# Which engine rounds the attention weights: 20 of 30 steps on ScalarE instead of 15

## The chip, the cores and the metric

The kernel runs on one NeuronCore of one Trainium2 chip. The metric is the device time of one execution in microseconds. Three runs of the kernel before gave 1110.03, 1110.61 and 1113.11 us; the median is 1110.61 us.

## The reference, cut to what matters

One layer over 1250 nodes of 768 features: a layer norm; a graph convolution over 20000 edges and an attention, both added to the input; then a mixture of experts on the normed sum. The change is in the attention, whose weights are a polynomial instead of an exponential:

```python
xn = _layernorm(x, axis=-1)
qkv = xn @ w_qkv + b_qkv          # 12 heads of 64
q, k, v = (qkv[0] * SCALE, qkv[1], qkv[2])
A = jnp.einsum('bhnd,bhmd->bhnm', q, k)
numerator = 1.0 + A + 0.5 * A * A
attn = numerator / numerator.sum(axis=-1, keepdims=True)
out = jnp.einsum('bhnm,bhmd->bhnd', attn, v)
x = x + gnn(xn, edge_index, W, b) + (out @ w_proj + b_proj)
x = x + experts(_layernorm(x))
```

The kernel computes the numerator as ((A + 1) squared + 1) / 2; the factor 1/2 drops out in the division.

## The kernel before, in words

It is written without a scheduler: each engine has its own program, written out by hand, and they meet at semaphores. Every float32 matmul is done as three products (or two) of operands that are cut into a rounded high part (type fp32r) and the low part that is left. So everything that TensorE (PE) reads has a high and a low tile: K is cut into KHA and KLA (KHB and KLB for the odd head), Q into the two halves of MA (MB), the weights of the attention into Ph and Pl.

The stages: norm, transposes and values V, up to 141 us; the attention, in six turns of one pair of heads each (`turn(j, last)`, five in a loop and the last one apart), 141 to 626 us; hidden features, edges and projection, then the experts.

A turn has 30 steps. Step i belongs to head a, to one of three chunks of 416 or 418 query columns, and to two tiles of 125 keys. One step is this chain:

1. PE, lines 1150 and 1151: scores, four matmuls into the PSUM buffer i % 2 (`sc_done`). They wait until the square of step i - 2 has emptied it.
2. ScalarE (ACT), line 834: Pf = (scores + 1) squared (`sq_done`). It waits for the scores and, three buffers round, for Pl of step i - 3.
3. The rounding: Ph = Pf + 1 as fp32r. On ACT it is line 812 (`round_weights`); on VectorE (DVE) it is line 1022. The list `HI_ON_ACT` of line 600 says which engine does it for which step.
4. DVE, line 1024: Pl = Pf + 1 - Ph (`p_lo`), always on DVE.
5. PE, line 1166: four matmuls of Ph and Pl with the values vsb, three steps later (LAG = 3).

All engines work strictly in the order of their programs. What matters for the change is where the rounding stands there. On DVE it stands in step i, right in front of Pl(i). On ACT the rounding of step i stands in round i + 1 of the loop, behind the square of step i + 1; that square in turn waits for the scores of step i + 1.

Between these steps lies other work, put at fixed steps by tables of numbers: the next pair's projections of Q and K (PE lines 1872 to 1874; read out by ACT 767 and 770), their high parts (ACT 779, 781) and low parts (DVE 894, 898), the splitting of the next weights (ACT 759, DVE 881), comparisons of edge keys (DVE 977), the folding of the output (ACT 821, DVE 955), the denominators (DVE 948, 950), and K turned round for a Gram matrix: PE transposes it in three groups at steps 24, 27 and 30 (line 1088), ACT takes the high part one round later (786), DVE the low part two rounds later (908), all through one PSUM bank. So PE may begin a group only when DVE's line 908 has finished the one before; the Gram matrix (line 1095, step 32) waits for the third. Behind it PE begins the next pair. The turn ends on DVE with the division and splitting of the output (lines 965 to 969).

Of the kernel before, what the change touches and what calls it, by code (L numbers as in the profile page):

```python
# [70 lines left out]
STEPS = 30  # L71
# [30 lines left out]
def build(nc, x, src, dst, gnn_w, gnn_b, w_qkv, b_qkv, w_proj, b_proj, sw, sb_, w1, b1, w2, b2, out,  # L102
          counts, keyd, vdram, odram, rows, x1d, invd, blank):
    ctx = ExitStack()
    with ctx:
# [491 lines left out]
                    pe.wait_ge(xt_lo, FIRST_UNIT[4])  # L597
                value(i)

        HI_ON_ACT = [i % 5 in (1, 3) or i in (0, 27, 29) for i in range(STEPS)]  # L600
        NA = sum(HI_ON_ACT)
        ND = STEPS - NA
        FREE = 1
# [152 lines left out]
        def _(act):  # L756
# [48 lines left out]
            def turn(j, last):  # L805
                def round_weights(i):

                    w = step(i)[4]
                    act.wait_ge(sq_done, j * STEPS + (i + 1))
                    if i >= RING:  # L810
                        act.wait_ge(pv_done, j * STEPS + (i - RING + 1))
                    act.activation(Ph[:, i % RING, :, 0:w], Pf[:, i % RING, :, 0:w], ACT.Identity,  # L812
                                   bias=1.0).then_inc(p_hiA, 1)
# [14 lines left out]
                for i in range(END):  # L828
                    if i < STEPS:
                        w = step(i)[4]  # L830
                        act.wait_ge(sc_done, j * STEPS + (i + 1))
                        if i >= RING:
                            act.wait_ge(p_lo, j * STEPS + (i - RING + 1))
                        act.activation(Pf[:, i % RING, :, 0:w], ps[0:T, 2 * (i % 2):2 * (i % 2) + 2, 0:w],  # L834
                                       ACT.Square, bias=1.0).then_inc(sq_done, 1)
                    if 1 <= i <= STEPS and HI_ON_ACT[i - 1]:
                        round_weights(i - 1)
# [40 lines left out]
        def _(dve):  # L878
# [56 lines left out]
            def turn(j, last):  # L935
# [61 lines left out]
                for i in range(END):  # L997
# [15 lines left out]
                    if i < STEPS:  # L1013
                        w = step(i)[4]
                        p, f, h = Pl[:, i % RING, :, 0:w], Pf[:, i % RING, :, 0:w], Ph[:, i % RING, :, 0:w]
                        if i >= RING:
                            dve.wait_ge(pv_done, j * STEPS + (i - RING + 1))
                        if HI_ON_ACT[i]:
                            dve.wait_ge(p_hiA, j * NA + (sum(HI_ON_ACT[:i]) + 1))
                        else:  # L1020
                            dve.wait_ge(sq_done, j * STEPS + (i + 1))
                            dve.tensor_scalar(h, f, 1.0, None, ALU.add).then_inc(p_hiD, 1)  # L1022
                            dve.wait_ge(p_hiD, j * ND + (i - sum(HI_ON_ACT[:i]) + 1))
                        dve.scalar_tensor_tensor(out=p, in0=f, scalar=1.0, in1=h.bitcast(F32), op0=ALU.add,  # L1024
# [880 lines left out]
```

## Time and profile before

| | |
|---|---|
| median of the runs | 1110.61 us |
| the profiled execution | 1114.51 us, of it 1112.6 us span |
| PE matmul busy | 933.1 us (84% of the span) |
| DVE busy | 773.2 us (69%) |
| ACT busy | 483.2 us (43%) |
| 225 to 305 us (pair 1 without its last 3 us): PE, DVE, ACT busy | 73.50, 68.48, 52.76 of 80 us |
| roundings L812 on ACT / L1022 on DVE | 90 / 90 |
| where the page's 40 slices show POOL idle | from slice 23 (612 us) to the experts |
| first scores of the six pairs | 140.97, 225.01, 307.91, 392.18, 474.84, 558.81 us |
| last values matmul of the last pair starts | 625.60 us |

Pairs are counted from 0, and so are steps. Pf(25) means the square of step 25, and in the same way Ph and Pl. In a line of the profile, "PE 0.48 [1.33 <-DVE kt L908]" means that the instruction was busy for 0.48 us and that its engine had been idle for 1.33 us before it, until DVE's line 908 released it. PE matmuls overlap at their ends (one starts each 0.19 us, though one takes 0.35). Also on DVE and ACT a following instruction often starts some 0.1 us before the shown end of the one before, so that the time one instruction takes out of an engine's day is best read from start to start.

### The profile page before, as it was taken

To read this page: it belongs to the slowest core of one execution; us is meant where nothing else is said; L and a number is where in the kernel's file an instruction comes from. 1 tells how busy PE (TensorE), PEld (TensorE's weight loads), DVE (VectorE), ACT (ScalarE), POOL (GpSimd) and SP (SyncE) were. 2 spreads that over 40 slices of the span, in tenths; PEclk is the share of its full clock that TensorE was granted. 3 is DMA by queue.
4 is the path that set the end of the run, shared out by engine and by line. 5 is a ranking of instruction groups with operands and counts; after the bars stand their busy time and mean duration, and the time that the engine had idled before them with its cause. 6 is when DMAs were issued, how large, how long until landed. Compare 5 with 4: busy or idle time off the path is not lost.

```text
span 1112.6 us, 15566 instructions
## 1 busy us (share of the span) xinstructions
PE 933.1 (84%) x5250; PEld 887.4 (80%) x5250; DVE 773.2 (69%) x1557; ACT 483.2 (43%) x710; POOL 342.0 (31%) x223
## 2 busy tenths in 40 slices
PE   3897789989989989989998779699999983197885
PEld 3896778878878978878987679699999982197885
DVE  6778168889878889878887635646676666067673
ACT  2221256656656656656667402112232222154540
POOL 2025555544546546534344000000000002323342
PEclk9898899999999999999999889899999995599898
DMA  8966443283273273285463374554545424786761
GB/s 235 350 181 144 85 88 49 36 153 56 28 153 49 35 153 52 32 173 118 120 133 70 47 164 108 135 134 110 146 114 144 109 70 152 214 268 213 232 223 45
DMA packets 139572, 142.44 MB, mean 128 GB/s; under 512 B 71418, under 2 KB 119133, under 8 KB 138503
## 3 DMA queue, kind: packets, MB, share of 16 engines
q1 hardware_dynamic: 110628, 125.01, 42.7%
q0 software_dynamic: 28496, 16.68, 10.3%
q8 instruction: 26, 0.43, 0.2%
q10 hardware_dynamic: 403, 0.17, 0.1%
q14 instruction: 19, 0.16, 0.0%
HBM read 99.09 MB, written 42.97 MB: 128 GB/s over the span
## 4 chain that ended last, share of the span: by engine, by line
PE 51%; DVE 16%; issue 12%; DMA 9%; ACT 8%; POOL 1%; SPq 1%; DVEq 0%; ACTq 0%; POOLq 0%
PE ps L1872 12%; PE ps L1874 11%; PE ps L1873 11%; PE ps L1166 6%; PE ps L1150 3%; PE ps L1151 3%; ACT Ph L812 3%; DMA out<-oE,ids 3%; DVE Pl L1024 3%; DMA vdram<-VS 3%; ACT Pf L834 2%; DVE Ph L1022 2%; PE ps L1520 1%; DMA Cs<-counts 1%; DVE oE L1806 1%
## 5 line engine op out<-in xcount | busy, mean ns | idle before, releaser
L372 POOL DMA_INDIRECT counts<-countc,idxu x157 | 273.5, 1742 | 299.8 <-DMA counts<-countc,idxu 204.7
L1024 DVE SCALAR_TENSOR_TENSOR Pl<-Pf,Ph 125x832 fp32r<-125x832 f32 (+1 forms) x180 | 184.4, 1026 | 65.0 <-ACT Ph L812 58.9
L834 ACT ACTIVATE Pf<-ps 125x832 f32<-125x832 f32 (+1 forms) x180 | 155.8, 866 | 147.1 <-PE ps L1151 140.1
L1166 PE MATMUL ps<-Ph,vsb 125*128 125x416 f32 (+1 forms) x360 | 132.1, 367 | 10.4 <-DVE Pl L1024 10.1
L1166 PE MATMUL ps<-Pl,vsb 125*128 125x416 f32 (+1 forms) x360 | 127.8, 355 | 0.0
L1663 POOL DMA_INDIRECT rows<-XF,slots x10 | 14.7, 1470 | 337.3 <-DVE slots L1479 334.6
L1872 PE MATMUL ps<-XH,wqkH 128*128 128x416 f32 (+1 forms) x216 | 81.3, 376 | 19.6 <-DVE R L942 9.9
L1872 PE MATMUL ps<-wH,XH 128*125 128x384 f32 x240 | 84.7, 353 | 10.5 <-DVE OHL L969 5.8
L1166 PEld LDWEIGHTS ps<-Ph,vsb 125*128 125x128 f32 x360 | 68.9, 191 | 20.7 <-DVE Pl L1024 10.6
L1873 PE MATMUL ps<-wL,XH 128*125 128x384 f32 x240 | 83.4, 348 | 0.0
L1874 PE MATMUL ps<-wH,XL 128*125 128x384 f32 x240 | 83.2, 346 | 0.0
L812 ACT ACTIVATE Ph<-Pf 125x832 fp32r<-125x832 f32 (+1 forms) x90 | 80.0, 896 | 0.7
L1150 PE MATMUL ps<-MA,KHA 128*125 128x416 f32 (+1 forms) x180 | 70.5, 392 | 10.6 <-DVE MA L898 10.6
L1874 PE MATMUL ps<-XH,wqkL 128*128 128x416 f32 (+1 forms) x216 | 78.0, 361 | 0.0
L1873 PE MATMUL ps<-XL,wqkH 128*128 128x416 f32 (+1 forms) x216 | 77.6, 359 | 0.0
L1872 PE MATMUL ps<-HH,CH 125*125 125x384 f32 x200 | 69.5, 347 | 7.4 <-DVE CL L1358 7.4
L1166 PEld LDWEIGHTS ps<-Pl,vsb 125*128 125x128 f32 x360 | 69.3, 193 | 0.9
L1873 PE MATMUL ps<-HL,CH 125*125 125x384 f32 x200 | 68.4, 342 | 0.0
L1874 PE MATMUL ps<-HH,CL 125*125 125x384 f32 x200 | 68.3, 341 | 0.0
L1150 PE MATMUL ps<-MB,KHB 128*125 128x416 f32 (+1 forms) x180 | 65.2, 362 | 0.7 <-ACT Pf L834 0.7
L1151 PE MATMUL ps<-MA,KLA 128*125 128x416 f32 (+1 forms) x180 | 64.5, 358 | 0.0
L1151 PE MATMUL ps<-MB,KLB 128*125 128x416 f32 (+1 forms) x180 | 63.9, 355 | 0.0
(247 smaller groups left out, 2243.5 us busy)
## 6 DMA issues: line engine op xcount, KB each, us to landing
Cs<-counts SPq DMA_DIRECT2D x20, 546.9 KB
w1s<-L_ffn_w SPq DMA_DIRECT2D x8, 1152.0 KB
w2s<-L_ffn_w SPq DMA_DIRECT2D x8, 1152.0 KB, 5.7
odram<-OHL SPq DMA_DIRECT2D x12, 625.0 KB, 8.5
oS<-odram SPq DMA_DIRECT2D x10, 750.0 KB, 4.8
vdram<-VS SPq DMA_DIRECT2D x10, 672.0 KB
vsb<-vdram SPq DMA_DIRECT2D x12, 560.0 KB
kt<-keyd SPq DMA_DIRECT2D x5, 1280.0 KB, 6.0
```

The source lines that it names most:

```text
L372: pool.indirect_dma_start(out=counts, out_offset=bass.IndirectOffsetOnAxis(ap=idxu[:, c:c + 1], axis=0), in_=countc[:, c:c + 1], in_offset ...
L812: act.activation(Ph[:, i % RING, :, 0:w], Pf[:, i % RING, :, 0:w], ACT.Identity, bias=1.0).then_inc(p_hiA, 1)
L834: act.activation(Pf[:, i % RING, :, 0:w], ps[0:T, 2 * (i % 2):2 * (i % 2) + 2, 0:w], ACT.Square, bias=1.0).then_inc(sq_done, 1)
L1022: dve.tensor_scalar(h, f, 1.0, None, ALU.add).then_inc(p_hiD, 1)
L1024: dve.scalar_tensor_tensor(out=p, in0=f, scalar=1.0, in1=h.bitcast(F32), op0=ALU.add, op1=ALU.subtract).then_inc(p_lo, 1)
L1150: pe.matmul(out_, KH[a][:, kt * T:(kt + 1) * T], q, start=True, stop=False)
L1151: ins = pe.matmul(out_, KL[a][:, kt * T:(kt + 1) * T], q, start=False, stop=True)
L1166: ins = pe.matmul(ps[:, 4 + s % 2, 0:w], vsb[:, 2 * kp + t, a, :], part[:, m % RING, t, 0:w], start=(kp == 0 and t == 0 and part is Ph), s ...
L1663: pool.indirect_dma_start(out=rows, out_offset=bass.IndirectOffsetOnAxis(ap=slots[:, i:i + 1], axis=0), in_=XF[:, i, :], in_offset=None, b ...
L1872: pe.matmul(out, lh, rh, start=(k == 0), stop=False)
L1873: pe.matmul(out, lh, rl, start=False, stop=False)
L1874: ins = pe.matmul(out, ll, rh, start=False, stop=(k == tiles - 1))
```

## The change

The list that gives the rounding to ACT is replaced by a regular pattern of three:

```diff
-        HI_ON_ACT = [i % 5 in (1, 3) or i in (0, 27, 29) for i in range(STEPS)]
+        HI_ON_ACT = [i % 3 != 2 for i in range(STEPS)]
```

Before, ACT rounded steps 0, 1, 3, 6, 8, 11, 13, 16, 18, 21, 23, 26, 27, 28 and 29, 15 in all. Now it rounds all but 2, 5, 8, ... 29, which makes 20. Ten steps go from DVE to ACT (4, 7, 9, 10, 12, 15, 19, 22, 24, 25) and five from ACT to DVE (8, 11, 23, 26, 29). `NA` and `ND`, the numbers of roundings of a turn by which the semaphores count, follow from the list. PE's instructions and their order are the same in both.

ACT's part of the program for rounds 25 and 26 of a turn (Pf(25) to the first instruction behind Pf(26)), before:

```order
L834 ACTIVATE Pf<-ps 125x2x416
L758 ISA
L759 ACTIVATE wqkH<-ws 128x768
L785 ISA
L786 ACTIVATE kt<-ps 125x4x128
L779 ACTIVATE KHA<-K 64x416
L831 REGISTER_ALU
L834 ACTIVATE Pf<-ps 125x2x416
L779 ACTIVATE KHA<-K 64x416
```

and now:

```order
L834 ACTIVATE Pf<-ps 125x2x416
L812 ACTIVATE Ph<-Pf 125x2x416
L758 ISA
L759 ACTIVATE wqkH<-ws 128x768
L785 ISA
L786 ACTIVATE kt<-ps 125x4x128
L779 ACTIVATE KHA<-K 64x416
L831 REGISTER_ALU
L834 ACTIVATE Pf<-ps 125x2x416
L812 ACTIVATE Ph<-Pf 125x2x416
L779 ACTIVATE KHA<-K 64x416
```

Ph(24) now stands behind Pf(25), in front of the weights' split, and Ph(25) behind Pf(26).

DVE's part of the program for steps 25 and 26, from the low parts of step 25 to Pl(26), before:

```order
L1021 REGISTER_ALU
L1022 TENSOR_SCALAR Ph<-Pf 125x2x416
L1023 REGISTER_ALU
L1024 SCALAR_TENSOR_TENSOR Pl<-Pf,Ph 125x2x416
L893 ISA
L894 TENSOR_TENSOR KLA<-K,KHA 64x418
L908 TENSOR_TENSOR kt<-ps,kt 125x4x128
L1017 REGISTER_ALU
L1024 SCALAR_TENSOR_TENSOR Pl<-Pf,Ph 125x2x416
```

and now:

```order
L1017 REGISTER_ALU
L1019 REGISTER_ALU
L1024 SCALAR_TENSOR_TENSOR Pl<-Pf,Ph 125x2x416
L893 ISA
L894 TENSOR_TENSOR KLA<-K,KHA 64x418
L908 TENSOR_TENSOR kt<-ps,kt 125x4x128
L1021 REGISTER_ALU
L1022 TENSOR_SCALAR Ph<-Pf 125x2x416
L1023 REGISTER_ALU
L1024 SCALAR_TENSOR_TENSOR Pl<-Pf,Ph 125x2x416
```

Pl(25), and with it line 908 of the first turned group behind it, now waits for ACT's Ph(25); the rounding in front of Pl(26) has come to DVE.

DVE's program for steps 28 and 29, from Pl(28) on, now (before, the same without the row L1022 and without the counting rows round it):

```order
L1024 SCALAR_TENSOR_TENSOR Pl<-Pf,Ph 125x2x416
L908 TENSOR_TENSOR kt<-ps,kt 125x4x128
L1021 REGISTER_ALU
L1022 TENSOR_SCALAR Ph<-Pf 125x2x416
L1023 REGISTER_ALU
L1024 SCALAR_TENSOR_TENSOR Pl<-Pf,Ph 125x2x416
L954 REGISTER_ALU
L955 TENSOR_TENSOR OUN<-ps,tmpo 64x416
```

The rounding of step 29 now stands on DVE, in front of all the work that ends a turn.

## Rows read from the trace of the kernel before

**Rows 1.** Groups of instructions by line: busy us, mean ns, idle before.

```profile
L812 ACT ACTIVATE Ph<-Pf 125x832 fp32r<-125x832 f32 (+1 forms) x90 | 80.0, 896 | 0.7
L1022 DVE TENSOR_SCALAR Ph<-Pf 125x832 fp32r<-125x832 f32 (+1 forms) x90 | 56.3, 625 | 6.3 <-DVE eqp L977 2.5
```

**Rows 2.** Waits from 225 to 308 us, one pair: us in total, times, longest.

```profile
PE ps L1872 <- DVE R L942: 2.0, 1, 2.0
...
PE ps L1150 <- DVE MA L898: 1.5, 1, 1.5
...
PE ps L1088 <- DVE kt L908: 1.3, 1, 1.3
PE ps L1166 <- DVE Pl L1024: 1.2, 2, 0.8
...
PE ps L1095 <- DVE kt L908: 1.2, 1, 1.2
```

**Rows 3.** Timeline of pair 1, steps 4 and 5: start, us, engine, line.

```profile
237.95 0.54 ACT L781 ACTIVATE MA<-Q 64x416 fp32r<-64x416 f32 x1
...
238.90 1.03 DVE L1024 SCALAR_TENSOR_TENSOR Pl<-Pf,Ph 125x836 fp32r<-125x836 f32 x1
```

**Rows 4.** Timeline of pair 1, steps 15 to 17.

```profile
269.37 0.60 DVE L1022 TENSOR_SCALAR Ph<-Pf 125x836 fp32r<-125x836 f32 x1
...
269.97 0.89 ACT L812 ACTIVATE Ph<-Pf 125x836 fp32r<-125x836 f32 x1
...
271.18 0.43 PE L1166 MATMUL ps<-Ph,vsb 125*128 125x418 f32 x1 [0.47 <-DVE Pl L1024]
...
271.35 1.03 DVE L1024 SCALAR_TENSOR_TENSOR Pl<-Pf,Ph 125x836 fp32r<-125x836 f32 x1
...
275.23 0.46 PE L1166 MATMUL ps<-Ph,vsb 125*128 125x418 f32 x1 [0.77 <-DVE Pl L1024]
```

**Rows 5.** Timeline of pair 1, steps 25 to 29, ACT alone.

```profile
288.36 0.87 ACT L834 ACTIVATE Pf<-ps 125x832 f32<-125x832 f32 x1 [0.73 <-PE ps L1151]
289.12 0.84 ACT L759 ACTIVATE wqkH<-ws 128x768 fp32r<-128x768 f32 x1
...
290.33 0.54 ACT L779 ACTIVATE KHA<-K 64x416 fp32r<-64x416 f32 x1
...
293.69 0.86 ACT L834 ACTIVATE Pf<-ps 125x832 f32<-125x832 f32 x1 [1.36 <-PE ps L1151]
294.45 0.89 ACT L812 ACTIVATE Ph<-Pf 125x832 fp32r<-125x832 f32 x1
295.24 0.60 ACT L770 ACTIVATE Q<-ps,pbias 128x418 f32<-128x418 f32 x1
295.73 0.87 ACT L834 ACTIVATE Pf<-ps 125x832 f32<-125x832 f32 x1
...
299.62 1.68 ACT L812 ACTIVATE Ph<-Pf 125x832 fp32r<-125x832 f32 x2
```

**Rows 6.** Timeline of pair 1, steps 25 to 30, DVE and PE.

```profile
292.03 1.03 DVE L1024 SCALAR_TENSOR_TENSOR Pl<-Pf,Ph 125x832 fp32r<-125x832 f32 x1
...
293.48 0.68 DVE L908 TENSOR_TENSOR kt<-ps,kt 125x512 fp32r<-125x512 f32 x1
...
294.25 0.66 PE L1088 MATMUL ps<-ident,K 128*125 128x128 f32 x4
...
300.65 1.03 DVE L1024 SCALAR_TENSOR_TENSOR Pl<-Pf,Ph 125x832 fp32r<-125x832 f32 x1 [1.12 <-ACT Ph L812]
...
302.19 1.02 DVE L1024 SCALAR_TENSOR_TENSOR Pl<-Pf,Ph 125x832 fp32r<-125x832 f32 x1
...
302.33 0.48 PE L1088 MATMUL ps<-ident,K 128*125 128x128 f32 x2 [1.33 <-DVE kt L908]
```

**Rows 7.** Timeline of the last pair's end, DVE and PE.

```profile
622.91 1.96 DVE L1024 SCALAR_TENSOR_TENSOR Pl<-Pf,Ph 125x832 fp32r<-125x832 f32 x2 [0.91 <-ACT Ph L812]
...
631.71 0.65 PE L1872 MATMUL ps<-wH,XH 128*125 128x384 f32 x1 [5.77 <-DVE OHL L969]
```

## The prediction

> **What bounds the kernel now.** I read the busy times by stretch first: in one pair's 80 us PE is busy for 92% of the time, DVE for 86% and ACT for 66% (73.50, 68.48 and 52.76 us). So PE sets the length of a pair, and a moved rounding only counts where it makes PE wait or spares it a wait. The list of waits for one pair [rows 2] gives those places. PE waits for DVE five times for more than a microsecond or so in sum: for R (2.0 us) and for MA (1.5 us) at steps 5 to 7, for Pl before the value matmuls (1.2 us, of it 0.47 at step 15 and 0.77 at step 17 [rows 4]), for the second turned group of K (1.3 us, in front of L1088 at step 30) and for the third (1.2 us, in front of L1095). The reader is to see that each wait has an instruction of DVE behind it, none of ACT. That speaks for relieving DVE; but DVE in turn sat idle for ACT's Ph in front of many a Pl, as in the row at 300.65 [rows 6]. The question at each place is thus which of the two engines is late, and I followed the timeline of pair 1 step by step. Pairs 0 to 4 repeat it within a few tenths.
>
> **What a moved rounding costs by itself.** On ACT 0.896 us, on DVE 0.625 us in the mean [rows 1]. Per pair ACT gets five more, 4.5 us, and has 27 of 80 us idle; DVE loses five, 3.1 us. No engine becomes the bound by its sum. The order decides: on ACT, Ph(i) comes behind Pf(i+1), on DVE right before Pl(i).
>
> Here the Trainium skill speaks against the direction: "Trainium Architecture — The Big Picture", section "The five engines, in one table", says that ScalarE is not for simple arithmetic and that VectorE is up to about 3 times faster per element. The rows give 0.896 to 0.625, a factor of 1.4 [rows 1]. By the page's full factor, an estimate, a rounding on ACT would take 3 x 0.625 = 1.9 us, and the two that lie on the path below would delay it by some 2 us more in each of five pairs, to 1128 or so. I go by the rows.
>
> **Steps 0 to 9.** Steps 0 to 3 are unchanged. Ph(4) goes to ACT behind Pf(5), where L781 starts now, at 237.95. It ends at 237.95 + 0.90 = 238.85, and Pl(4) can start at 238.88; it starts at 238.90 now [rows 3]. So the waits for MA and R stay as they are: 0. Ph(7) and Ph(9) make Pl(7) and Pl(9) later by 0.9 and 0.3 us, which PE does not feel (their value matmuls started 4.0 and 1.3 us after Pl's end). Ph(8) on DVE makes Pl(8) 1.2 us earlier, which PE does not need either.
>
> **Steps 10 to 22.** This is where the gain is. DVE gives up Ph(15), which stands at 269.37 [rows 4], so Pl(15) is ready some 0.65 us earlier and the 0.47 us wait before the values of step 15 goes. The next in line is Pl(16). It cannot follow by 0.65: it needs ACT's Ph(16), which ended at 269.97 + 0.89 = 270.86 and is now 0.07 later, since Ph(15) and a read-out stand in front of Pf(17). Pl(16) starts at 270.96 instead of 271.35 [rows 4], 0.39 earlier, and so do Ph(17) and Pl(17), for which PE waited 0.77 [rows 4]. So of 1.24 us of waits 0.4 us is really won, the rest turns into a wait at step 17. In two pairs of five a wait of 0.12 at step 10 goes as well. I take 0.45 us per pair; the bounds are 0 and 1.3. The moved Ph(12), Ph(19), Ph(22) find ACT idle enough.
>
> **Steps 24 to 27, a new wait.** Ph(24) and Ph(25) go to ACT. Before, ACT's chain was Pf(25) at 288.36, split of the weights at 289.12, high parts until 290.33 + 0.54 = 290.87, then idle until Pf(26). Now Ph(24) starts at 289.12 and takes 0.79 of ACT's time (from start to start, as 294.45 to 295.24); split, turned K and KHA follow, 1.75 us, until 291.66; then Pf(26), and 0.76 later (as 293.69 to 294.45) Ph(25), at 292.42, which ends at 293.31 [rows 5]. Pl(25) started at 292.03 and can now start at 293.34: 1.31 us later. DVE's L908 behind it was done at 293.48 + 0.68 = 294.16, just in time for PE's L1088 at 294.25 [rows 6]. It is now done at 295.47, and L1088 starts at 295.53 (0.06 behind, as at 302.27 and 302.33). PE loses 1.28 us. PE being earlier by the 0.45 helps nothing here, since ACT's chain starts with the scores of step 25 and is earlier by as much.
>
> Does it come back? PE runs into the next wait at 301.00 (1.33 us idle before 302.33) [rows 6], which could swallow a delay. It does not: that wait ends with L908, behind Pl(28), behind ACT's Ph(28) (1.12 us idle before 300.65) [rows 6], and ACT works from Pf(28) at 295.73 to Ph(28) at 299.62 without a gap [rows 5]. Pf(28) starts with the scores of step 28, which PE issues behind the delayed L1088. So the whole chain is 1.28 later. Ph(26), which leaves ACT, stood in front of it, but Pf(28) waited for the scores anyway.
>
> **Step 29.** Ph(29) goes from ACT to DVE, behind L908 and in front of Pl(29), which now starts at 302.19 [rows 6]. From there DVE works without a gap of more than 0.16 us until the third L908, for which PE waits in front of L1095 [rows 2]. The rounding takes 0.62 us of DVE, and all of it is added: 0.62 us per pair.
>
> **The last pair.** It has no projections, so PE waits for Pl nearly throughout, and ACT and DVE take turns in being late. I followed it in the same way: in steps 7 to 22 Pl comes up to 0.6 us earlier, but the inverse of the denominators (behind Ph(13), unchanged) and the three large weight splits on both engines catch this up, and Pl(26) to Pl(28) start as now, held by ACT. At the end Ph(29) on DVE splits the two Pl [rows 7]; DVE works without a gap from there to the end of the turn, for which PE waits (5.77 us idle) [rows 7]. So +0.62; the bounds are -3.1 (all five roundings) and +3.
>
> **The sum.** 5 x (1.28 + 0.62 - 0.45) = 7.25, and 0.62 for the last pair: 7.9 us. The scatter of edges on POOL is over by 612 us (POOL's digit in the page's slices is 0 from there), before the attention ends, so it adds nothing; the stages behind the attention are the same and only start later. Against the profiled execution's 1114.5 us this makes 1122.4. That execution was 3.9 us above the median, and I take the difference over to the median: 1110.6 + 7.9 = 1118.5 us.
>
> **The rivals.**
> 1. DVE's relief wins. For it: all of PE's long waits have a DVE line behind them [rows 2]. If the waits for Pl went wholly (1.24 per pair), nothing were added at the end of a turn, and the last pair gained 3.1: -9.3, 1101.3 us. Against it: Pl(16) needs ACT, and Ph(29) is plainly added to DVE's chain.
> 2. No new wait before L1088, because ACT's queue clears in another order than I reckon, or L908 has slack. Then 5 x (0.62 - 0.45) + 0.62 = +1.5, 1112.1 us, no change that can be told. Against it: the margin now is 294.25 - 294.16 = 0.09 us.
> 3. ACT becomes late more often: nothing is won at steps 15 and 17, since each Ph now follows another Ph, and the last pair, where ACT has less slack, pays 3 us. 5 x 1.90 + 3 = +12.5, 1123.1 us. For it: in the last pair steps of PE need 1.5 us, and square and rounding on ACT 1.6.
>
> **How the numbers follow.** Forecast 0.60, rival 1 0.10, rival 2 0.17, rival 3 0.13. A measurement of this kernel can tell about 0.3%, 3.3 us. The forecast lies beyond this unless its sum is wrong by more than half, which I give a tenth of its chance or less. Slower: 0.55 + 0.13 + a little of rival 2 = 0.70; same: 0.05 + 0.14 = 0.19; faster 0.11. The range: the forecast with its bounds goes from +3 to +12; to leave out no more than a fifth it has to take in most of rival 2 and rival 3 up to its price: 1109.5 to 1124.
>
> **What would show it.** In the changed kernel's profile: 120 of L812 and 60 of L1022; in each of the five pairs a wait of about 1.3 us of PE before the L1088 of step 27 (four matmuls), which isn't there now; the wait at step 30 as long as now; L1095 and the next pair's first scores later by about 1.45 us, so that a pair takes 84.3 us instead of 82.9; the wait at step 15 gone and that at step 17 still there. It is wrong if the L1088 of step 27 starts without a wait, or if pairs do not get longer.

## The result and the profile after

The changed kernel takes 1125.99 us (median of 4 runs) against 1111.46 us before (4 runs, the three above and one beside the changed kernel): 14.5 us slower. The ratio, which is one of means here and below, is 1.014, 95% interval 1.010 to 1.018. Run again in the last series it came to 1.0129 (1.0106 to 1.0151). The forecast said slower by 7.9 us, 1118.5 with a range up to 1124. So the direction and most of the mechanism were right, the forecast size was little more than half of the measured one, and the time lies 2 us above the range.

Groups of instructions by line in the changed kernel (busy us, mean ns, idle before; they answer to [rows 1]):

```profile
L812 ACT ACTIVATE Ph<-Pf 125x832 fp32r<-125x832 f32 (+1 forms) x120 | 107.4, 895 | 0.8
L1022 DVE TENSOR_SCALAR Ph<-Pf 125x832 fp32r<-125x832 f32 (+1 forms) x60 | 37.4, 624 | 3.3
```

The change does what it says: 120 and 60 roundings, at the same price each. Now the busy times of pair 1 from its first scores to the next pair's, first of the kernel before:

```profile
225.01:307.91 82.90, 75.24 (x397) 70.06 (x396) 71.16 (x136) 53.62 (x78) 41.19 (x23) 1.00 0.46 80
```

and of the changed kernel (columns: length, then busy us of PE, PE's weight loads, DVE, ACT and POOL, the granted clock, the busy share of the DMA engines and GB/s):

```profile
228.12:312.68 84.56, 75.46 (x398) 70.14 (x397) 67.45 (x131) 57.01 (x83) 39.83 (x24) 1.00 0.44 78
```

PE is busy for 75.2 and 75.5 us, both at full clock (1.00 is the 2.4 GHz level). DVE has 3.7 us less to do, ACT 3.4 more, and the pair is 1.66 us longer: nearly all of it is waiting (PE's idle time grows by 1.44 us, its busy time by 0.22). The waits of PE in that pair of the changed kernel (us in total, times, longest), which answer to [rows 2]:

```profile
PE ps L1088 <- DVE kt L908: 2.2, 2, 1.2
...
PE ps L1872 <- DVE R L942: 2.0, 1, 2.0
PE ps L1095 <- DVE kt L908: 1.8, 1, 1.8
...
PE ps L1150 <- DVE MA L898: 1.5, 1, 1.5
...
PE ps L1872 <- ACT K L767: 0.7, 1, 0.7
PE ps L1166 <- DVE Pl L1024: 0.7, 1, 0.7
```

Against [rows 2]: R and MA as before. Pl 0.7 instead of 1.2. L1088 waits twice instead of once, 0.9 us more: the new wait of step 27 is 1.0 us, that of step 30 is 1.2 instead of 1.3. L1095 waits 0.6 us more. And there is a line that the kernel before doesn't have: L1872 waits 0.7 us for ACT's L767. It is PE's wait at step 24, before the next projection:

```profile
285.75 0.87 ACT L834 ACTIVATE Pf<-ps 125x832 f32<-125x832 f32 x1 [1.02 <-PE ps L1151]
286.52 0.89 ACT L812 ACTIVATE Ph<-Pf 125x832 fp32r<-125x832 f32 x1
287.43 0.52 ACT L821 ACTIVATE tmpo<-ps 64x418 f32<-64x418 f32 x1
287.97 0.61 ACT L767 ACTIVATE K<-ps,pbias 128x416 f32<-128x416 f32 x1
...
288.73 0.46 PE L1872 MATMUL ps<-XH,wqkH 128*128 128x418 f32 x1 [0.74 <-ACT K L767]
```

Read it from below: PE may write the next projection only when ACT has read the last one out of the one PSUM bank (line 767, which then signals `kq_full`). The read-out stands in round 23, behind Pf(23), now behind Ph(22) too, and behind the fold. The tail, which answers to [rows 5] and [rows 6]:

```profile
291.39 0.87 ACT L834 ACTIVATE Pf<-ps 125x832 f32<-125x832 f32 x1 [1.53 <-PE ps L1151]
292.15 0.89 ACT L812 ACTIVATE Ph<-Pf 125x832 fp32r<-125x832 f32 x1
...
294.15 0.54 ACT L779 ACTIVATE KHA<-K 64x416 fp32r<-64x416 f32 x1
294.59 0.86 ACT L834 ACTIVATE Pf<-ps 125x832 f32<-125x832 f32 x1
295.33 0.90 ACT L812 ACTIVATE Ph<-Pf 125x832 fp32r<-125x832 f32 x1
...
296.26 1.03 DVE L1024 SCALAR_TENSOR_TENSOR Pl<-Pf,Ph 125x832 fp32r<-125x832 f32 x1 [1.54 <-ACT Ph L812]
...
298.44 0.70 PE L1088 MATMUL ps<-ident,K 128*125 128x128 f32 x4 [1.02 <-DVE kt L908]
...
304.76 1.03 DVE L1024 SCALAR_TENSOR_TENSOR Pl<-Pf,Ph 125x832 fp32r<-125x832 f32 x1 [1.34 <-ACT Ph L812]
...
306.30 0.58 DVE L1022 TENSOR_SCALAR Ph<-Pf 125x832 fp32r<-125x832 f32 x1
306.44 0.48 PE L1088 MATMUL ps<-ident,K 128*125 128x128 f32 x2 [1.21 <-DVE kt L908]
...
306.92 1.05 DVE L1024 SCALAR_TENSOR_TENSOR Pl<-Pf,Ph 125x832 fp32r<-125x832 f32 x1
```

ACT goes from Pf(25) to Ph(25) without a gap; Pl(25) waits for it, L1088 of step 27 waits behind it, and the wait of step 30 is still there in spite of that (1.21, before 1.33).

An idle time in these lists begins at the shown end of the last matmul, 0.35 us after its start, though the next one could have started after 0.19. What a wait costs is therefore better read from the first scores of one step to those of the next. In pair 1 step 24 is 0.79 us longer than before (idle 0.74) and step 27 1.22 us (idle 1.02); steps 24 to 28 together take 12.58 us instead of 10.59.

Where the time went, pair by pair (first scores to first scores; the last one to the end of its last values):

| us | pair 0 | 1 | 2 | 3 | 4 | 5 |
|---|---|---|---|---|---|---|
| before | 84.04 | 82.90 | 84.27 | 82.67 | 83.97 | 67.13 |
| changed | 86.15 | 84.56 | 86.56 | 84.62 | 86.21 | 68.85 |

The attention is 12.0 us longer, 10.3 in the five looped pairs and 1.7 in the last. Pairs 0, 2 and 4 hold, in both kernels, one stretch of 3.4 us at a granted clock of half speed (1.2 GHz). It begins in step 7, behind the waits for MA and R, and lies mostly in steps 8 to 11. Steps 7 to 11 of the kernel before, first with the stretch (pair 0), then without (pair 1):

```profile
156.06:172.38 16.32, 14.35 (x70) 13.35 (x68) 11.59 (x24) 8.40 (x12) 8.64 (x7) 0.90 0.31 41
240.00:254.76 14.76, 12.80 (x70) 11.97 (x68) 11.62 (x23) 8.40 (x12) 5.96 (x3) 1.00 0.59 113
```

So a stretch costs some 1.55 us there, in both kernels alike. Pairs 1 and 3 are free of it; where a pair of an experiment is called "clean" below, it has none either. The last pair holds one stretch in both kernels too, but not at the same place: at step 21 before, at step 24 now. It takes part in the 1.7 us of the last pair, as the run with the old list there shows below.

### The profile page after: what moved, and what is told of

Same layout as the page of the kernel before. It is cut to its first block, busy times and chain, and to the rows that moved or that the text cites. A ratio compares the mean times of both kernels' runs of the same rounds, so it can differ in the third digit from the quotient of the medians.

```text
span 1124.2 us, 15616 instructions
## 1 busy us (share of the span) xinstructions
PE 939.2 (84%) x5250; PEld 892.8 (79%) x5250; DVE 756.1 (67%) x1527; ACT 503.7 (45%) x740; POOL 342.4 (30%) x223
## 4 chain that ended last, share of the span: by engine, by line
PE 53%; DVE 15%; issue 11%; ACT 9%; DMA 9%; POOL 1%; SPq 1%; DVEq 1%; ACTq 0%; POOLq 0%
PE ps L1872 12%; PE ps L1874 11%; PE ps L1873 11%; PE ps L1166 7%; ACT Ph L812 4%; PE ps L1150 4%; PE ps L1151 3%; DMA out<-oE,ids 3%; DMA vdram<-VS 3%; ACT Pf L834 2%; DVE Pl L1024 2%; DVE Ph L1022 1%; PE ps L1520 1%; DVE oE L1806 1%; PE ps L1126 1%
## 5 line engine op out<-in xcount | busy, mean ns | idle before, releaser
L1663 POOL DMA_INDIRECT rows<-XF,slots x10 | 14.7, 1470 | 337.6 <-DVE slots L1479 334.8
L812 ACT ACTIVATE Ph<-Pf 125x832 fp32r<-125x832 f32 (+1 forms) x120 | 107.4, 895 | 0.8
L1872 PE MATMUL ps<-XH,wqkH 128*128 128x416 f32 (+1 forms) x216 | 82.1, 380 | 23.3 <-DVE R L942 9.9
L1872 PE MATMUL ps<-wH,XH 128*125 128x384 f32 x240 | 85.7, 357 | 10.4 <-DVE OHL L969 5.8
L1874 PE MATMUL ps<-wH,XL 128*125 128x384 f32 x240 | 83.8, 349 | 0.0
L1150 PE MATMUL ps<-MA,KHA 128*125 128x416 f32 (+1 forms) x180 | 70.6, 392 | 10.5 <-DVE MA L898 10.5
L1872 PE MATMUL ps<-HH,CH 125*125 125x384 f32 x200 | 69.5, 347 | 7.4 <-DVE CL L1358 7.4
L1872 PEld LDWEIGHTS ps<-XH,wqkH 128*128 128x128 f32 x216 | 42.1, 195 | 29.2 <-issue 20.7
```

The lines of the kernel that those rows point to most:

```text
L1150: pe.matmul(out_, KH[a][:, kt * T:(kt + 1) * T], q, start=True, stop=False)
L1663: pool.indirect_dma_start(out=rows, out_offset=bass.IndirectOffsetOnAxis(ap=slots[:, i:i + 1], axis=0), in_=XF[:, i, :], in_offset=None, b ...
L1872: pe.matmul(out, lh, rh, start=(k == 0), stop=False)
L1874: ins = pe.matmul(out, ll, rh, start=False, stop=(k == tiles - 1))
```

## The experiments

Theory A says that each loss hangs on one place, where a certain rounding stands in front of something that PE waits for. Rival B says that it is load: ACT has more to do, so the number of roundings counts. The intervals of the ratios reach 0.2 to 0.5% to either side, so for single waits the trace decides; "list" is the set of steps on ACT, N that of the changed kernel and O that of the one before.

**The missed wait, by order alone.** N, with the read-out in front:

```diff
+                    if not last and i == 23:
+                        read_kq(j + 1, 2)
                     if 1 <= i <= STEPS and HI_ON_ACT[i - 1]:
                         round_weights(i - 1)
```

(and round 23 left out further down).

> The changed kernel with ACT's third read-out of K (line 767 of round 23) in front of Ph(22) and the fold; nothing else moves, the load of every engine is the same. Theory A (places): PE's wait of 0.74 us before L1872 at step 24, which the forecast missed, goes, since the read-out can start at once behind Pf(23); the waits at steps 27 and in front of L1095 stay. Five pairs by about 0.7: 3 to 4 us faster than the changed kernel, about 1122. Rival B (load): ACT has as much to do as before, so the time stays at 1126 and the 0.74 us turn up somewhere else in the pair, behind Ph(22).

Measured 1124.08 us, 1.011 (1.006 to 1.016). Its waits of PE in a pair (line numbers are 2 higher here, L1090 is L1088):

```profile
PE ps L1090 <- DVE kt L910: 2.2, 2, 1.2
...
PE ps L1874 <- DVE R L944: 1.9, 1, 1.9
...
PE ps L1097 <- DVE kt L910: 1.8, 1, 1.8
```

The wait for L767 is gone from the list in all five pairs, and the others stayed within 0.25 us of the changed kernel's; from step 24 to 28 a pair needs 11.56 us instead of 12.58 (10.5 to 10.6 before). The loads are the same. So the place decides here, not the load. The time itself can't tell the two theories apart: it is 1.9 us below the changed kernel's, not 3 to 4, and the trace has six half-clock stretches in the looped pairs instead of three, which take back most of the 5 us won.

**Ph(25) back on DVE.** N without 25: `i % 3 != 2 and i != 25`.

> The changed kernel with Ph(25) back on DVE. Theory A: L908 of step 26 comes about 1 us earlier, PE's wait before L1088 at step 27 (1.02 us) goes, each of five pairs is 0.9 to 1.0 us shorter: about 1121. Rival B (one moved rounding is worth its share of the load, 15 roundings' worth of loss divided by ten): 1 us or so in all, 1125. Rival C (the wait is hidden anyway by the one at step 30): the step 30 wait grows by 1.0, time 1126.

In the trace the wait of step 27 fell from 1.0 to 0.13 us (0.40 in one pair), and that of step 30 stayed at 1.21, so rival C falls: it does not swallow it. Steps 24 to 28 took 11.7 instead of 12.58 us (11.97 in that one pair). But the time was 1128.48 us, 1.015 (1.010 to 1.019), no faster than the changed kernel. Its trace has 163.7 us at half clock against 156.1 in the changed kernel's; the looped pairs hold nearly six stretches instead of three, four of them at the seams between pairs, behind the waits at step 30 and before L1095. At some 1.5 us each the additional ones take back the 4.1 us won in the five pairs. The expected time did not come out, though the wait went as expected.

**Ph(29) back on ACT.** N with 29: `i % 3 != 2 or i == 29`.

> The changed kernel with Ph(29) back on ACT. Theory A: DVE's end of each turn is 0.62 us earlier, PE's wait before L1095 falls from 1.8-2.0 to about 1.3, all six pairs 0.6 us shorter: 3.7 us, about 1122. Rival: Ph(29) on ACT comes as late as on DVE, since it follows Ph(28) there (Pl(29) starts within 0.1 us of where it does now), no change: 1126.

The wait before L1095 fell from between 1.8 and 2.0 us to 1.15 in all pairs, as theory A says, 0.6 to 0.85 each; steps 28 to the end took 13.14 us instead of 13.8 to 14.0. Time 1125.88 us, 1.012 (1.008 to 1.016), where 1122 was expected: the gain doesn't show in it. Here every looped pair holds a stretch, five instead of three.

**Only the last pair as before.** A list of its own for the last turn, on ACT and DVE:

```diff
+                HI_ON_ACT = OLD if last else NEW
```

> The changed kernel, but the last pair (turn 5) has the old list. It splits the loss by place. Theory A: the last pair falls from 68.84 to 67.1 us, 1.7 us in all, pairs 0 to 4 are as in the changed kernel: about 1124.3. Rival: half of the loss or more is in the last pair or comes from outside the attention (the forecast had 0.62 for it); then more than 3 us come back or none.

Measured 1125.52 us, 1.012 (1.008 to 1.017). The loss is thus in the looped pairs for the most part; a gain of 1.7 us is too small for this comparison of times. The last pair took 69.19 us, longer than in either kernel, as it holds two half-clock stretches here, 36.1 and 53.1 us after its first scores. It can be compared with last pairs that have the new list and two stretches within 0.7 us of the same places: 69.73 us in the yardstick below, 69.95 in the run with the read-out in front. So the list costs the last pair 0.5 to 0.8 us. The other 1.0 or so of the 1.7 goes with the place of the stretch: in the kernel before it falls on step 21, and PE's wait for Pl(20) behind it is 1.28 us instead of the 2.03 of the runs whose list is the old one at these steps and whose stretch comes later.

**Three of the ten moves undone.** `i % 3 != 2 and i not in (22, 25) or i == 29`, 19 of 30 on ACT.

> The changed kernel with Ph(22) and Ph(25) back on DVE and Ph(29) back on ACT (19 of 30 on ACT). Theory A (the loss hangs on these three places, not on the number of roundings on ACT): the waits of 0.74 us at step 24 and of 1.0 at step 27 go and the one before L1095 falls to 1.15-1.3; a pair without a half-clock stretch takes about 82.3 us, a little less than before, since the middle of the pair keeps its gain of 0.5; the time is within 0.3% of before. Rival B (load): 19 roundings on ACT cost nearly what 20 do, 1.01 of before.

Measured 1112.77 us, 1.0009 of before (0.9992 to 1.0025, 12 runs). Its waits in a pair:

```profile
PE ps L1872 <- DVE R L942: 2.0, 1, 2.0
...
PE ps L1150 <- DVE MA L898: 1.4, 1, 1.4
PE ps L1088 <- DVE kt L908: 1.2, 1, 1.2
PE ps L1095 <- DVE kt L908: 1.1, 1, 1.1
...
PE ps L1166 <- DVE Pl L1024: 0.7, 1, 0.7
```

That is the list of before with a shorter last line (a wait of 0.1 us at step 27 is left). Clean pairs take 82.1 to 82.2 us, 0.5 to 0.8 less than before; the time doesn't show this, and the traced execution was the fastest of the twelve. With 19 roundings on ACT the loss of 20 is gone: rival B falls, and the three places together are all of the loss that the time can show.

**Each term alone, in the kernel before.** O with 22, and O with 24 and 25 (the list gets 24 and 25 in the same way; 26 stays on ACT):

```diff
-        HI_ON_ACT = [i % 5 in (1, 3) or i in (0, 27, 29) for i in range(STEPS)]
+        HI_ON_ACT = [i % 5 in (1, 3) or i in (0, 22, 27, 29) for i in range(STEPS)]
```

> The kernel before with Ph(22) alone moved to ACT: the missed term by itself. Theory A: K's third read-out (L767 of round 23) comes 0.8 us later behind Ph(22), and PE's projection of step 24 now waits 0.7 to 0.8 us for it in each of five pairs, as in the changed kernel; nothing gives it back: pairs 0.7 longer, 1.003 of before. Rival (the wait only shows up there because the middle of the pair had got faster): PE comes to step 24 no earlier than in the kernel before, the wait is 0.2 us or less and the time is the same.

Measured 1118.06 us, 1.0057 (1.0036 to 1.0079). PE's wait for L767 is there, 0.74 us in each of the five pairs:

```profile
PE ps L1872 <- ACT K L767: 0.7, 1, 0.7
```

One moved step, five instructions in the looped pairs, costs half a per cent. Step 24 is 0.8 us longer in all five; the one clean pair takes 83.24 us, 0.3 to 0.6 above before, as shorter waits before that gave some back. Of the 6.0 us the five waits are 4.0, and the trace has one stretch more in the looped pairs.

> The kernel before with Ph(24) and Ph(25) moved to ACT, the forecast's main term by itself. Theory A: PE waits 1.0 to 1.3 us before L1088 of step 27 in each of five pairs, the wait of 1.3 at step 30 stays, and the pair is 1.0 to 1.4 us longer: 1.005 of before. Rival (the delay is swallowed by the wait at step 30): that wait shrinks to 0.3, the time is the same.

Measured 1122.85 us, 1.0104 (1.0079 to 1.0128). The wait of step 27 is 1.0 us in all five pairs, that of step 30 stays at 1.21; steps 24 to 28 take 11.79 us instead of 10.5 to 10.6. The swallowing rival falls again. The time, 10.8 us longer, is more than these 1.2 us per pair explain; where the rest comes from is open.

**The last pair.** N without 12, a single execution (1126.08 us), so only its trace counts.

> The changed kernel with Ph(12) back on DVE. It tests the last pair, where the forecast had 0.6 us and the trace 1.7. Theory A: Ph(12) stands in front of the low-level work of round 13 on ACT and so delays Pf(14) by 0.9 us and Ph(13) behind it; PE waits 0.81 us for Pl(13) in the last pair. With Ph(12) on DVE that wait goes and the last pair is about 0.5 to 0.8 us shorter; pairs 0 to 4 unchanged. Rival: the wait comes from Ph(10) and Ph(9) before it; it stays.

In the changed kernel PE waits 0.81 us for Pl(13) in the last pair; here this wait is gone, and the pair takes 69.22 us. The yardstick below, with two half-clock stretches in the same places, takes 69.73: 0.5 less, the lower end of what was expected. So PE's wait for Pl(13) does hang on Ph(12). The chain in the changed kernel: Ph(12) at 598.22, high part and fold, Pf(14) only at 600.26 though its scores were ready at 599.38, Ph(13) at 601.15.

**The yardstick.**

> The changed kernel itself once more, as the yardstick of this job: the same chip and the same runs of the kernel before as the two parts. The traces give 10 us (2.0 for each of five pairs) and 1.7 for the last pair: 11 to 12 us, 1.010 to 1.011. The first measurement said 1.014 (1.010 to 1.018). If the time beyond the waits is real (more stretches at half clock), it is above 1.013 again and its trace shows more than the four such stretches; if it was scatter, it comes out at 1.009 to 1.012.

1126.73 us, 1.0129 (1.0106 to 1.0151), with five stretches in the attention instead of four. It lies just between the two outcomes set apart beforehand. That the loss is larger than the waits give is thus likely, but not shown: both intervals take in 12 to 13 us, by which the attention got longer in the two traces.

The traces also allow a comparison that the scatter of the times does not touch, an estimate: from the length of the five looped pairs take off 1.55 us for each half-clock stretch in them. A looped pair then takes 82.6 us before, 84.7 in the changed kernel, in the yardstick and in the run with the old list in the last pair, 83.5, 83.8 and 83.9 with one place undone (read-out in front, 25, 29), and 82.2 with three moves undone (22, 25, 29). The three gains of 1.2, 0.9 and 0.8 add up to 2.9, and together they gave 2.5. Each of these runs has one trace, so whether undoing a place brings on more stretches (6, nearly 6 and 5 in the three runs, against 3, 3 and 2 in the three traces with the new list in the looped pairs) stays open.

**Towards a better list.** By the places where PE waits: O with 15 and 17; O without 0 and 1; both, and 28 on DVE.

```diff
+        HI_ON_ACT = [i % 5 in (1, 3) or i in (0, 15, 17, 27, 29) for i in range(STEPS)]
+        HI_ON_ACT = [i % 5 in (1, 3) and i != 1 or i in (27, 29) for i in range(STEPS)]
+        HI_ON_ACT = [i in (3, 6, 8, 11, 13, 15, 16, 17, 18, 21, 23, 26, 27, 29) for i in range(STEPS)]
```

> The kernel before with only Ph(15) and Ph(17) moved to ACT. Theory A: PE's waits of 0.48 at step 18 and 0.47-0.77 at step 20 go and nothing is added: each of five pairs 1.0 to 1.2 us shorter, 0.995 of before. Rival: with Ph(15) and Ph(17) both behind a square, ACT is late with Ph(16) or Ph(18) instead and the wait stays at about 0.6 as in the changed kernel: a gain of 0.5 per pair, 0.998.

1108.44 us, 0.9958 (0.9939 to 0.9976). The waits for Pl are gone in the looped pairs, but for 0.1 us at step 10 in two of them; clean pairs take 81.3 to 82.0 us. Two more roundings on ACT make the kernel faster.

> The kernel before with Ph(0) and Ph(1) moved to DVE (13 of 30 on ACT), the opposite direction. Theory A: DVE idles at the start of a pair for ACT's Ph(0) and Ph(1) (0.93 and 1.37 us); without this Pl(1), the low part of Q and R come 0.7 to 1.1 us earlier, PE's wait of 1.5 us at step 5 shrinks by that and the one at step 7 stays: 0.7 to 1.1 us per pair, 0.995 of before. Rival B (load: DVE is the busier engine, so each rounding put on it costs): slower by 0.6 per rounding and pair, 1.006.

1108.57 us, 0.9963 (0.9947 to 0.9979). Two more on the busier DVE make it faster as well, by as much. In the looped pairs behind the first the wait for MA falls from 1.5 us to between 0.8 and 1.0, and the one for R grows from 2.0 to between 2.2 and 2.5; steps 0 to 8 of a clean pair take 19.6 to 19.7 us instead of 19.9. That is 1 us or so of the 3.9. The trace also has one half-clock stretch in the looped pairs instead of three; with these taken off as above a looped pair takes 82.1 us instead of 82.6. How much of the gain is the moves' own is thus not settled.

> The kernel before with Ph(15), Ph(17) on ACT and Ph(0), Ph(1), Ph(28) on DVE (14 of 30 on ACT), chosen by the places where PE waits. Theory A: the gains add up: 1.1 in the middle, 0.7 to 1.1 at the start and 0.4 at step 30 (L908 behind Pl(28) comes earlier) per pair, 2.2 to 2.6 us each in five pairs: 0.989 of before. Rival: each gain turns into the next wait (the one at step 7 and the one before L1095 grow), at most half of it is left: 0.995.

1107.33 us, 0.9944 (0.9923 to 0.9965), faster than both kernels, but half of what adding up gave, as the rival says. Its waits in a clean pair of 80.96 us:

```profile
PE ps L1872 <- DVE R L942: 2.3, 1, 2.3
...
PE ps L1095 <- DVE kt L908: 1.1, 1, 1.1
PE ps L1088 <- DVE kt L908: 1.0, 1, 1.0
PE ps L1150 <- DVE MA L898: 0.9, 1, 0.9
```

No Pl is left in this pair; MA and L1088 gave 0.6 and 0.3, and R took 0.3 back. Four of the five looped pairs hold a stretch here.

## Why the prediction was right or wrong, point by point

- *Steps 0 to 9: nothing.* Right: MA 1.5 and R 2.0 in both.
- *Steps 10 to 22: a gain of 0.45 per pair, of 1.24.* Right: Pl waits 0.66 us in pair 1 instead of 1.24 (0.47 and 0.77), and what is left is the wait at step 17. A wait of 0.12 at step 10 and 0.17 of the one for the inverse went too. By the first scores of step 24 the five pairs are 0.36, 0.87, 0.37, 0.79 and 0.55 us ahead, 0.59 in the mean.
- *"The moved Ph(12), Ph(19), Ph(22) find ACT idle enough."* This is the step that failed. ACT was idle enough for its own sake, but the sentence asked only who waits for Ph and Pl, not who waits for what stands behind Ph on ACT. Behind Ph(22) stands the read-out of K, and PE waits for that: 0.74 us in each looped pair, 0.80 by the length of step 24. The wait comes with this move alone (the run with 22 alone) and goes by order alone (the run with the read-out in front). The forecast put this term at nothing; it is 4.0 us in the five pairs. Behind Ph(12) stand a high part, a fold and Pf(14): PE waits 0.81 us in the last pair, of which taking the move back gave 0.5.
- *Steps 24 to 27: a new wait of 1.28 before L1088, not swallowed at step 30.* Right, in size too: step 27 is 1.21 to 1.33 us longer, 1.26 in the mean (the list shows 1.02 of it as idle), with step 30 at 1.21.
- *Step 29: 0.62 per pair before L1095.* Right: the wait before L1095 is 1.77 to 2.01 instead of 1.14 to 1.22, and from step 28 to its end a pair is 0.5 to 0.7 us longer, 0.60 in the mean.
- *The last pair: +0.62.* The traces show 1.7, but the list's own share is 0.5 to 0.8; the rest goes with the place of a half-clock stretch, for which the forecast had no term. That the size fits is partly luck, since its terms were not the forecast's. Ph(29) in front of the last Pl came as forecast (PE waits 0.55 us for Pl(29), before not at all). The wait at step 16 was overlooked, and the wait for Pl(26), which was to start as before, grew from 0.76 to 1.39: it stays at 1.39 in the run with 29 back on ACT, and in all runs that leave Ph(26) on ACT it is 0.8. Against these stand some 0.6 us won at step 10 and 0.6 at step 22 (yardstick against the run with the old list).
- *The sum.* A looped pair was to be 1.45 longer. It is 2.05 longer in the mean (1.66 and 1.95 in the clean pairs, 2.1 to 2.3 in the others): -0.59 until step 24, then 0.80, 1.26 and 0.60. So without the missed 0.80 the looped pairs would have been 1.25 longer, 1 us less in all than forecast. Of the 6.6 us by which 14.5 exceeds 7.9, the missed wait is 4.0, the other terms of the looped pairs are -1.0, and the last pair is 1.1; 2.5 are left.
- *The rest, 2.5 us.* They are not in the attention. The profiled execution of before was 3 us above its median and that of the changed kernel at its median; I had carried the first difference over to the forecast as if it belonged to both. The traces have 142, 156 and 165 us at half clock (before, changed, yardstick), 10 us of the difference in the stage before the attention, which is the same program in all. That share is not one trace's scatter: the granted clock is 0.931 and 0.933 in the mean of the four and five executions of the changed kernel, and 0.936 to 0.937 in those of the kernel before that ran beside the experiments. But it doesn't explain the time either, since the run with the old list in the last pair has 0.937 and took 1125.5 us. As both intervals take in 12 us, the 2.5 may be scatter. This stays open, as does whether longer or other waits bring on such stretches: no run fixed the clock.
- *Rivals.* The faster one was wrong: DVE's relief alone gives nothing where PE waits for something behind ACT. That a gain can be had by choosing the places, 0.4% with 15 and 17, the runs showed. The price of rival 3 (1123.1) was nearest to the time, but not its mechanism: steps 15 and 17 did win.

## What to carry to other kernels

When work moves to an idle engine, list for every moved instruction what stands behind it in that engine's program and who waits for that, read-outs of a shared PSUM bank first; that the engine is idle for a third of the time does not answer it. Moves in both directions gained here (0.4% each), so neither the number of moved pieces nor the busy shares decided here, but the place. Measure what a wait costs from step to step, not by the idle time alone (1.26 against 1.02 us here). And count the half-clock stretches before comparing two times or two traces: at 1.5 us each, three of them hid the 4 to 5 us that a single place gave back. A forecast that adds up single waits from one trace should carry a range for them and for how the profiled run stands to the median.

## What the runs showed of the hardware

- A rounding on ACT took 0.895 us for 125 x 832 float32 elements and 0.78 to 0.81 from its start to the next instruction's start where that was ready; on DVE 0.57 to 0.88, median 0.60.
- With PE busy for some 90% of a looped pair and no wait longer than 2.6 us, the granted clock still fell to half for 3.4 us, always behind a pair of waits (MA and R, or step 30 and L1095), in one (without 0 and 1) to six (read-out in front, 25 on DVE) places of the looped pairs; in the whole attention of the 14 traces it was 2 to 8 stretches. A whole stretch behind MA and R made steps 7 to 11 1.4 to 1.7 us longer (14.7 to 14.9 us without, 16.3 to 16.5 with, in the runs that leave 0 and 1 as they were). In the last pair, where it fell on steps that wait anyway, it cost less.
